# Both ends of the state-space scan in a four-stage token tower: when the second softplus, the last gate, the last products and the output projection are issued

## The chip, the cores and the metric

One of the eight cores of one Trainium2 chip runs the whole kernel. The metric is device time in microseconds (us), the median of several executions. Five engines take part, each with an instruction stream of its own, in order: TensorE (PE in the profile; its weight loads are PEld), VectorE (DVE), ScalarE (ACT), GpSimd (POOL), and SyncE (SP), which only issues transfers here. They meet through semaphores: an instruction adds to one when it is done, and another engine waits until the count is reached.

## The reference, cut to what matters

A tower of five layers over 32 sequences of 64 tokens with 1024 channels. A token layer makes h. Attention, a feed-forward layer with 4-bit weights, a selective state-space layer and a router with low-rank experts are then each added to h. The change touches the state-space layer alone, and the final store of the output:

```
proj = layernorm(h) @ W_in.T ; u, gate = split(proj)          # 2048 channels each
u = silu(conv4(u) + conv_b)
dt, B, C = split(u @ Wx.T) ; each rms-normed                   # 64, 16, 16
delta = softplus(dt @ Wdt.T + dt_bias)
for every token t, channel d and state n (16):
    state = exp(delta * A) * state + (delta * u) * B[n]
    y[t, d] += state * C[n]
y = (y + u * D) * silu(gate)
h = h + y @ W_out.T
```

## The kernel before, in words

The tokens are worked on in four blocks of 512 tokens (nblk = 4, loop over b on each engine). A tile has 128 channels on the partitions and 512 tokens along the row. The state-space layer of a block has four stretches.

*Input projection and gate strips.* A weight strip (1024 x 128) is loaded by SP into one of two raw buffers. ScalarE rounds it to a high part wh (`split`, L642), GpSimd subtracts to get the low part wl (L522), and TensorE makes 24 matmuls of it: high by high, low by high, high by low (`strip`, L947). There are four slots for split strips, so the split of strip i waits until strip i - 4 is used up. Strips WIN0.. make u; strips GATE0..GATE0+15 make the sixteen gate tiles. For gate tile m, VectorE scales psg[m % 2] by rstd in place (L1771), ScalarE takes the Silu into gt[m % 2] (L819) and stores gt to the DRAM tensor `gates` (L822), and strip m of TensorE waits until gate m - 2 has left its bank. Between the gates ScalarE does other work at fixed tiles m. That is soft(0), the softplus of channel tile 0, at m = 7; the diagonal at 9; settled(0), the copy of delta, at 10; transposed(0) at 11; and decay(0, 0) and decay(0, 1), the exponentials, at 12 and 14. Exponentials and the Silu are in different tables, so a switch of tables (ACT_TABLE_LOAD) stands on each side. The delta matmuls (`delta`) of tiles 0 and 1 are issued by TensorE at m = 7 and m = 11.

*The scan.* Sixteen channel tiles m, each with eight steps g (two of the sixteen states in each step). Step g: TensorE puts the drive terms into psx (`drives`, L1198; two buffers, so drives of step g + 1 wait for the scan of g - 1). VectorE runs the recurrence (`scan`, L1746) over 1024 columns from dA and psx into wst. GpSimd multiplies wst by C (L561). TensorE sums over the states into psg banks 0 and 1 (`sums`, L1214), three steps behind the drives. dA and wst have three slots of two steps (RING = 3), so scans wait for ScalarE's decay (L784) and for the sums of six steps before. Between its scans VectorE does soft_sum(m + 1) and drive_sum(m + 1), four small operations (L1718, L1719, L1728, L1729), on what ScalarE's soft(m + 1) (L737 to L744) wrote. When all sums of m are in, ScalarE copies them to twin (`parts`, L775), TensorE folds the two halves together (`finals`, L1233), ScalarE copies the result to u (`summed`), and GpSimd multiplies by the gate that SP loaded back (`gated`, L553). The last tile's gate product is VectorE's (L1735).

*Output projection.* When all sixteen gated tiles are there, ScalarE rounds them to yh (L869), VectorE subtracts to get yl (L1790), and TensorE makes eight output tiles, each from two strips: `strip_over_two` for the even ones (L1017, L1022), two calls of `strip` for the odd ones. VectorE adds each to h (L1796). yh[0..7] lie over the matrices dgB that the drives read, yh[8..15] over dA slots 0 and 1, yl[0..3] over dA slot 2 and yl[4..15] over the three slots of wst. gt lies over one of the two buffers of twin and one of gin.

*Order.* Every stream is written out by hand; there is no planner. The SP queue loads strips, then waits for all gates to be stored, then alternates gin and wdt loads. After the last product it loads h back (2 MB). At the end of the kernel one transfer of 2 MB stores the last block's h (L510).

## Time and profile before

| | us |
|---|---|
| median of 3 runs (lowest, highest) | 4074.54 (4069.95, 4077.92) |
| the profiled execution, device time | 4075.14 |
| its span, first to last instruction | 4073.3 |
| PE busy | 3868.0 (95%) |
| DVE busy | 2674.6 (66%) |
| POOL busy | 2235.6 (55%) |
| ACT busy | 2057.9 (51%) |
| mean granted TensorE clock | 0.983 of full |

The span is the time from the first to the last instruction; 1.8 us of the device time lie around it. Busy shares are means over stretches with different limits. In the projections TensorE never stops, while in the scan TensorE, VectorE and GpSimd are all close to full and take turns at holding the others up. So the places to read are the two seams, from the gate strips into the scan and from the scan into the output projection, which come four times each.

### The profile page before, as it was taken

To read this page: it belongs to the slowest core of one execution; us is meant where nothing else is said; L and a number is where in the kernel's file an instruction comes from. 1 tells how busy PE (TensorE), PEld (TensorE's weight loads), DVE (VectorE), ACT (ScalarE), POOL (GpSimd) and SP (SyncE) were. 2 spreads that over 40 slices of the span, in tenths; PEclk is the share of its full clock that TensorE was granted. 3 is DMA by queue.
4 is the path that set the end of the run, shared out by engine and by line. 5 is a ranking of instruction groups with operands and counts; after the bars stand their busy time and mean duration, and the time that the engine had idled before them with its cause. 6 is when DMAs were issued, how large, how long until landed. Compare 5 with 4: busy or idle time off the path is not lost.

```text
span 4073.3 us, 59277 instructions
## 1 busy us (share of the span) xinstructions
PE 3868.0 (95%) x22816; PEld 2542.0 (62%) x22816; DVE 2674.6 (66%) x2922; ACT 2057.9 (51%) x3012; POOL 2235.6 (55%) x972
## 2 busy tenths in 40 slices
PE   4899999999999999999999999999999999999998
PEld 1568777444678777544577877644377877744466
DVE  6965562999356563799635565499835557299943
ACT  7842344777232343777433233577633234477732
POOL 0023343999533343799733434599943443389952
PEclk7999999999999999999999999999999999999999
DMA  4242234000322224200132223400132223400022
GB/s 113 78 145 83 83 113 158 10 16 15 116 99 84 73 92 153 71 16 16 66 108 99 83 68 122 143 13 16 40 109 99 78 88 104 157 29 16 15 85 73
DMA packets 96697, 320.18 MB, mean 79 GB/s; under 512 B 12353, under 2 KB 16705, under 8 KB 91841
## 3 DMA queue, kind: packets, MB, share of 16 engines
q1 hardware_dynamic: 80320, 275.70, 20.6%
q10 hardware_dynamic: 16128, 41.03, 3.0%
q8 instruction: 173, 2.83, 0.3%
q14 instruction: 76, 0.61, 0.1%
HBM read 272.51 MB, written 44.17 MB: 78 GB/s over the span
## 4 chain that ended last, share of the span: by engine, by line
PE 35%; issue 32%; DVE 20%; POOL 11%; ACT 1%; POOLq 0%; ACTq 0%; DVEq 0%
PE psg L947 20%; DVE sb_wst L1746 17%; POOL sb_wl L522 9%; PE psx L1198 4%; PE psg L1017 3%; POOL sb_wst L561 2%; PE psg L1214 2%; PE psg L1022 1%; PE psx L1246 1%; DVE psg L1719 1%; DVE psg L1718 1%; PE psg L1317 1%; PE psx L964 0%; PE psg L1173 0%; DVE sb_rt L1834 0%
## 5 line engine op out<-in xcount | busy, mean ns | idle before, releaser
L522 POOL TENSOR_TENSOR sb_wl<-sb_raw,sb_wh 128x1024 fp32r<-128x1024 f32 x388 | 959.1, 2476 | 1760.0 <-ACT sb_wh L642 1759.7
L1746 DVE TENSOR_TENSOR_SCAN sb_wst<-sb_dA,psx 128x1024 f32<-128x1024 f32 x512 | 1130.2, 2268 | 9.4 <-PE psx L1198 7.4
L642 ACT ACTIVATE sb_wh<-sb_raw 128x1024 fp32r<-128x1024 f32 x388 | 407.5, 1053 | 558.7 <-PE psg L947 227.6
L784 ACT ACTIVATE sb_dA<-sb_dlt,sb_a_sb 128x504 f32<-128x504 f32 x1024 | 647.0, 705 | 51.8 <-DVE sb_wst L1746 49.6
L1198 PEld LDWEIGHTS psx<-sb_dgB,sb_duT 64*128 64x128 f32 x4096 | 360.4, 188 | 462.5 <-DVE sb_wst L1746 323.4
L1198 PE MATMUL psx<-sb_dgB,sb_duT 64*128 64x256 f32 x4096 | 587.4, 406 | 51.0 <-DVE sb_wst L1746 49.4
L1214 PE MATMUL psg<-sb_wst,sb_cst 64*64 64x512 f32 x4096 | 611.6, 623 | 17.3 <-POOL sb_wst L561 16.4
L561 POOL TENSOR_TENSOR sb_wst<-sb_wst,sb_cb_hi 128x1024 f32<-128x1024 f32 x256 | 596.1, 2362 | 29.9 <-DVE sb_wst L1746 29.5
L561 POOL TENSOR_TENSOR sb_wst<-sb_wst,sb_cb_lo 128x1024 f32<-128x1024 f32 x256 | 600.7, 2371 | 10.6 <-DVE sb_wst L1746 10.2
L947 PE MATMUL psg<-sb_xh,sb_wh 128*128 128x512 f32 x2080 | 532.1, 398 | 12.6 <-POOL sb_wl L522 7.1
L947 PE MATMUL psg<-sb_xh,sb_wl 128*128 128x512 f32 x2080 | 515.6, 390 | 0.0
L947 PE MATMUL psg<-sb_xl,sb_wh 128*128 128x512 f32 x2080 | 514.0, 389 | 0.0
L947 PEld LDWEIGHTS psg<-sb_xh,sb_wh 128*128 128x128 f32 x2080 | 382.6, 188 | 107.1 <-issue 15.3
L947 PEld LDWEIGHTS psg<-sb_xh,sb_wl 128*128 128x128 f32 x2080 | 390.3, 188 | 82.5
L947 PEld LDWEIGHTS psg<-sb_xl,sb_wh 128*128 128x128 f32 x2080 | 390.6, 188 | 81.1
L1214 PEld LDWEIGHTS psg<-sb_wst,sb_cst 64*64 64x64 f32 x4096 | 125.1, 133 | 208.6 <-issue 208.4
L1771 DVE TENSOR_TENSOR psg<-psg,sb_rstd 128x512 f32<-128x512 f32 x64 | 44.8, 700 | 316.0 <-PE psg L947 316.0
L1796 DVE TENSOR_TENSOR sb_h<-sb_h,psg 128x512 f32<-128x512 f32 x32 | 22.0, 688 | 257.3 <-PE psg L947 135.5
L1708 DVE SCALAR_TENSOR_TENSOR sb_cv<-psg,sb_conv,sb_cv 128x504 f32<-128x504 f32 (+2 forms) x192 | 141.0, 735 | 27.8 <-DVE sb_cv L1706 4.1
L775 ACT ACTIVATE sb_twin<-psg 128x512 f32<-128x512 f32 x128 | 69.5, 595 | 172.1 <-PE psg L1222 172.1
L693 ACT ACTIVATE sb_ah<-sb_ao 128x512 fp32r<-128x512 f32 x32 | 20.2, 632 | 193.3 <-DVE sb_ao L1664 193.3
L650 ACT ACTIVATE sb_xh<-sb_xc 128x512 fp32r<-128x512 f32 x128 | 79.1, 618 | 76.5 <-DVE sb_xc L1547 66.6
(274 smaller groups left out, 4959.8 us busy)
## 6 DMA issues: line engine op xcount, KB each, us to landing
sb_raw<-in_w SPq DMA_DIRECT2D x360, 512.0 KB, 3.5
sb_raw<-w_ffn_dequantized SPq DMA_DIRECT2D x32, 512.0 KB, 3.3
gates<-sb_gt ACTq DMA_DIRECT2D x64, 256.0 KB, 2.2
sb_gin<-gates SPq DMA_DIRECT2D x64, 256.0 KB, 2.7
h_after_tok<-sb_h SPq DMA_DIRECT2D x4, 2048.0 KB, 8.9
sb_cb_lo<-c_rows ACTq DMA_DIRECT2D x8, 1024.0 KB, 6.3
sb_cb_hi<-c_rows ACTq DMA_DIRECT2D x8, 1024.0 KB, 7.4
sb_h<-h_after_tok SPq DMA_DIRECT2D x4, 2048.0 KB, 7.7
```

The costliest lines, as they stand in the source:

```text
L522: pool.tensor_tensor(rest(b, i0), raw[:, i0 % RAW, :, :], high(b, i0).bitcast(F32), ALU.subtract).then_inc(s_wl, 1)
L561: pool.tensor_tensor(x, x, cb, ALU.mult).then_inc(s_p, 1)
L642: A(high(b, i0), raw[:, i0 % RAW, :, :], ACT.Copy).then_inc(s_wh, 1)
L650: A(xh[:, k, :], xc[:, k, :], ACT.Copy).then_inc(s_xh, 1)
L775: ins_ = A(twin[:, r, :], psg[:, r, :], ACT.Copy)
L784: ins_ = A(dA[:, (m * NQ + k) % RING, :, n, 1:S], dlt[:, m % 2, :].rearrange("p (b s) -> p b s", b=NB)[:, :, 1:S], ACT.Exp, scale=a_sb[:, ...
L947: ins_ = mm(psg[:, bank, :], w_[:, s_, k, :], x_[:, k0 + k, :], start=start and n == 0, stop=stop_ and n == 3 * KC - 1)
L1017: mm(psg[:, bank, :], w_[:, slot(b, i0 + s), k, :], X[:, k + KC * s, :], start=(k == 0 and n == 0 and s == 0), stop=False)
L1198: ins_ = mm(psx[:, 2 * j + r, :].rearrange("p (a t e) -> p a t e", a=8, e=2)[:, :, :, e], duT[r0:r0 + 64, m % 2, i * P:(i + 1) * P], dgB[r ...
L1214: ins_ = mm(psg[64 * c:64 * c + 64, r, :], C("fold")[r0:r0 + 64, :], wst[r0:r0 + 64, (m * NQ + k) % RING, :, 2 * half + c, :], start=(k == ...
L1708: ins_ = stt(y[:, :, d:S], x[:, :, 0:S - d], tap(3 - d), y[:, :, d:S], ALU.mult, ALU.add)
L1746: v.tensor_tensor_scan(wst[:, x, 4 * j:4 * j + 4, :, :].rearrange("p b n s -> p (b n s)"), dA[:, x, 4 * j:4 * j + 4, :, :].rearrange("p b ...
```

## The change

It does five things.

- VectorE's product. In channel tile 15 the last two C products (TAIL = 2, steps 6 and 7) are made by VectorE after the last scan (`product`, semaphore s_pd), and GpSimd makes six.
- The second softplus. soft(1), settled(1), soft_sum(1) and drive_sum(1) are issued among the gate strips, at m = 12, 14, 13 and 13, rather than in tile 0 of the scan.
- The last gate. The Silu of gate 15 and its store are issued by ScalarE after decay(0, 3), inside the scan. VectorE scales it from PSUM into gt[1], so that its bank is free. VectorE also clears dA's slot 2, which GpSimd did after waiting for the stored gates.
- The output projection. ScalarE copies yh in an order of its own (YH_ORDER) as soon as the drives, and then the scans, are done. TensorE begins the high parts of output tile 0 in bank 3 between the last sums, then does tile 1's highs in bank 1, then both lows. The other six tiles are made by two calls of `strip` each, in a loop.
- The store. The last block's h is stored in four transfers of two tiles each as the tiles are finished.

```diff
+YH_ORDER = list(range(KC)) + [12, 13, 8, 9, 10, 11, 14, 15]
+YL_ORDER = [0, 1, 2, 3, 8, 9, 10, 11, 12, 13, 4, 5, 6, 7, 14, 15]
+YH_AT = {k: n for n, k in enumerate(YH_ORDER)}
+YL_AT = {k: n for n, k in enumerate(YL_ORDER)}
+TAIL = 2
...
+                    for m in range(2):
+                        sp.wait_ge(s_dm, b * DC + m + 1 + CR_DM)
+                        sp.dma_start(wdt[:, m, :], ins["wdt"][m + 2]).then_inc(s_wdt[m], 16)
...
-                        if m < DC - 2:
+                        if 2 <= m < DC - 2:
...
-                    sp.wait_ge(s_p, b * DC * G + DC * G)
+                    sp.wait_ge(s_p, (b + 1) * (DC * G - TAIL))
...
+                if stop >= 5 and b == nblk - 1:
+                    for m in range(0, KC, 2):
+                        sp.wait_ge(s_upd, b * UPDS + 24 + m + 2 + CR_UPD)
+                        sp.dma_start(out[b, :, m:m + 2, :], h[:, m:m + 2, :]).then_inc(s_out, 16)
...
-                    for q in range(2):
-                        pool.wait_ge(s_gst[q], b * (16 * (DC // 2)) + 16 * (DC // 2) + 16)
                     pool.wait_ge(s_cb, 16 * NQ * (b + 1))
-                    settle(pool)
-                    pool.memset(dA[:, 2:RING, :, :, :].rearrange("p k b n s -> p (k b n) s")[:, :, 0:1], 0.0).then_inc(s_z, 1)
                     def gated(m):
...
-                        for g in range(G):
+                        for g in range(G - TAIL if m == DC - 1 else G):
...
+                    pool.wait_ge(s_pd, (b + 1) * TAIL)
...
+                    def gate(m, x):
                         act.wait_ge(s_gr, b * DC + m + 1)
                         act.wait_ge(s_gst[m % 2], b * 16 * (DC // 2) + m // 2 * 16 + 16)
-                        A(gt[:, m % 2, :], psg[:, m % 2, :], ACT.Silu).then_inc(s_gt, 1)
+                        A(gt[:, m % 2, :], x, ACT.Silu).then_inc(s_gt, 1)
                         act.wait_ge(s_gt, b * DC + m + 1 + CR_GT)
                         settle(act)
                         act.dma_start(gates[b, m], gt[:, m % 2, :]).then_inc(s_gst[m % 2], 16)
+                    for m in range(DC):
...
+                        if m < DC - 1:
+                            gate(m, psg[:, m % 2, :])
...
-                        if m in (12, 14):
+                        if m == 12:
                             act.preload_act_table_set(LN_EXP)
+                            soft(1)
                             act.wait_ge(s_zr, b + 1)
-                            decay(0, m // 2 - 6)
-                    act.preload_act_table_set(LN_EXP)
+                            decay(0, 0)
+                        if m == 14:
+                            act.preload_act_table_set(LN_EXP)
+                            settled(1)
+                            decay(0, 1)
                     for m in range(DC):
-                        if m < DC - 1:
+                        if 1 <= m < DC - 1:
                             soft(m + 1)
                         if m == 0:
                             act.wait_ge(s_z, b + 1)
                         decay(m, 2)
+                        if m == 1:
+                            for q in range(2):
+                                act.wait_ge(s_gst[q], b * (16 * (DC // 2)) + 16 * (DC // 2) + 16)
                         if m >= 1:
                             parts(m - 1)
                         decay(m, 3)
+                        if m == 0:
+                            gate(DC - 1, gt[:, 1, :])
+                            act.preload_act_table_set(LN_EXP)
+                        if 1 <= m < DC - 1:
+                            settled(m + 1)
                         if m < DC - 1:
-                            settled(m + 1)
                             decay(m + 1, 0)
                             transposed(m + 1)
                             decay(m + 1, 1)
...
                                 summed(m - 1)
                             diagonal(m + 1)
                     summed(DC - 2)
+                    def y_high(ms):
+                        for m in ms:
+                            act.wait_ge(s_y, b * DC + m + 1 + CR_Y)
+                            A(yh[:, m, :], u[:, m, :], ACT.Copy).then_inc(s_yh, 1)
+                    act.wait_ge(s_ur, (b + 1) * DC * G)
+                    y_high(YH_ORDER[0:10])
+                    act.wait_ge(s_scan, (b + 1) * DC * G + CR_SCAN)
+                    y_high(YH_ORDER[10:14])
+                    split(b, WOUT0 + AHEAD)
+                    y_high(YH_ORDER[14:15])
                     parts(DC - 1)
-                    act.wait_ge(s_y, (b + 1) * DC + CR_Y)
-                    for m in range(DC):
-                        A(yh[:, m, :], u[:, m, :], ACT.Copy).then_inc(s_yh, 1)
-                    for i in range(WOUT0 + AHEAD, BASE0 + 2 if stop >= 5 else LA0):
+                    y_high(YH_ORDER[15:16])
+                    for i in range(WOUT0 + AHEAD + 1, BASE0 + 2 if stop >= 5 else LA0):
...
+                            if k == 0 and m == 0:
+                                pe.wait_ge(s_gt, b * DC + DC - 1 + CR_GT)
+                            if m == DC - 1 and k == NQ - 1:
+                                pe.wait_ge(s_pd, (b + 1) * TAIL)
+                            else:
+                                pe.wait_ge(s_p, b * (DC * G - TAIL) + m * G + 2 * k + 2)
...
+                    def out_highs(m, bank, ks):
+                        for k in ks:
+                            i = WOUT0 + 2 * m + k // KC
+                            if k in (YH_ORDER[0], YH_ORDER[KC]):
+                                pe.wait_ge(s_wl, b * NSTRIP + i + 1 + CR_WL)
+                            pe.wait_ge(s_yh, b * DC + YH_AT[k] + 1)
+                            for n, w_ in enumerate((wh, wl)):
+                                mm(psg[:, bank, :], w_[:, slot(b, i), k % KC, :], yh[:, k, :],
+                                   start=(k == YH_ORDER[0] and n == 0), stop=False)
+                    def out_lows(m, bank):
+                        for k in range(DC):
+                            pe.wait_ge(s_yl, b * DC + YL_AT[k] + 1)
+                            ins_ = mm(psg[:, bank, :], wh[:, slot(b, WOUT0 + 2 * m + k // KC), k % KC, :], yl[:, k, :],
+                                      start=False, stop=(k == DC - 1))
+                            if k % KC == KC - 1:
+                                ins_.then_inc(s_strip, 1)
...
+                            if g == G - 1 and m == DC - 1:
+                                out_highs(0, 3, YH_ORDER[0:4])
                             sums_due(m * G + g - 3)
                             if g == 4 and m < DC - 1:
                                 transposes(m + 1)
                             if g == 4 and m >= 1:
                                 finals(m - 1, m < DC - 1)
-                    for step in range(DC * G - 3, DC * G):
+                    sums_due(DC * G - 3)
+                    out_highs(0, 3, YH_ORDER[4:5])
+                    for step in range(DC * G - 2, DC * G):
                         sums_due(step)
+                    out_highs(0, 3, YH_ORDER[5:8])
                     pe.wait_ge(s_yc, b * (DC - 1) + DC - 1)
                     finals(DC - 1, False)
-                    with loop(pe, 4) as jj:
+                    out_highs(0, 3, YH_ORDER[8:16])
+                    out_highs(1, 1, YH_ORDER)
+                    out_lows(0, 3)
+                    out_lows(1, 1)
+                    settle(pe)
+                    with pe.Fori(1, 4) as jj:
                         for q in range(2):
                             upd(b, 16 + jj * 2 + q - 1)
-                            if q == 0:
-                                strip_over_two(b, WOUT0, jj, 0, yh, yl,
-                                           (lambda k: pe.wait_ge(s_yh, b * DC + k + 1),
-                                            lambda k: pe.wait_ge(s_yl, b * DC + k + 1)))
-                            else:
-                                strip(b, WOUT0 + 2, jj, q, yh, yl, True, False)
-                                strip(b, WOUT0 + 3, jj, q, yh, yl, False, True, KC)
+                            strip(b, WOUT0 + 2 * q, jj, q, yh, yl, True, False)
+                            strip(b, WOUT0 + 2 * q + 1, jj, q, yh, yl, False, True, KC)
...
+                        if m < DC - 1:
+                            tt(psg[:, m % 2, :], psg[:, m % 2, :], rstd[:, :], ALU.mult).then_inc(s_gr, 1)
+                        else:
+                            v.memset(dA[:, 2:RING, :, :, :].rearrange("p k b n s -> p (k b n) s")[:, :, 0:1], 0.0).then_inc(s_z, 1)
+                            v.wait_ge(s_gst[1], b * 16 * (DC // 2) + m // 2 * 16 + 16)
+                            tt(gt[:, 1, :], psg[:, m % 2, :], rstd[:, :], ALU.mult).then_inc(s_gr, 1)
                         if m == 3:
                             prm_norm()
                         if m == 5:
...
                             v.memset(dA[:, 0:2, :, :, :].rearrange("p k b n s -> p (k b n) s")[:, :, 0:1], 0.0).then_inc(s_zr, 1)
                             soft_sum(0)
                             drive_sum(0)
+                        if m == 13:
+                            soft_sum(1)
+                            drive_sum(1)
                     for m in range(DC):
                         for g in range(G):
                             scan(m, g)
-                            if g == 1 and m < DC - 1:
+                            if g == 1 and 1 <= m < DC - 1:
                                 soft_sum(m + 1)
-                            if g == 3 and m < DC - 1:
+                            if g == 3 and 1 <= m < DC - 1:
                                 drive_sum(m + 1)
+                    def product(g):
+                        x = wst[:, (DC * NQ - 1) % RING, 4 * (g % 2):4 * (g % 2) + 4, :, :].rearrange("p b n s -> p (b n s)")
+                        cb = cb_hi[:, 1, 4 * (g % 2):4 * (g % 2) + 4, :, :].rearrange("p b n s -> p (b n s)")
+                        v.wait_ge(s_scan, b * DC * G + (DC - 1) * G + g + 1 + CR_SCAN)
+                        tt(x, x, cb, ALU.mult).then_inc(s_pd, 1)
+                    def y_low(ks):
+                        for k in ks:
+                            v.wait_ge(s_yh, b * DC + YH_AT[k] + 1)
+                            tt(yl[:, k, :], u[:, k, :], yh[:, k, :].bitcast(F32), ALU.subtract).then_inc(s_yl, 1)
+                    v.wait_ge(s_p, (b + 1) * (DC * G - TAIL))
+                    for g in range(G - TAIL, G):
+                        product(g)
+                    y_low(YL_ORDER[0:4])
+                    v.wait_ge(s_acc, (b + 1) * DC * NQ - 2)
+                    y_low(YL_ORDER[4:8])
+                    v.wait_ge(s_y, b * DC + DC - 1 + CR_Y)
                     gated(DC - 1)
-                    for m in range(DC):
-                        v.wait_ge(s_yh, b * DC + m + 1)
-                        tt(yl[:, m, :], u[:, m, :], yh[:, m, :].bitcast(F32), ALU.subtract).then_inc(s_yl, 1)
+                    v.wait_ge(s_acc, (b + 1) * DC * NQ)
+                    y_low(YL_ORDER[8:16])
...
-                        tt(hk(m), hk(m), psg[:, m % 2, :], ALU.add).then_inc(s_upd, 1)
+                        tt(hk(m), hk(m), psg[:, m % 2 if m else 3, :], ALU.add).then_inc(s_upd, 1)
```

## Rows read from the trace of the kernel before

**Rows 1.** The page: shares of the chain that ended last, by engine.

```profile
PE 35%; issue 32%; DVE 20%; POOL 11%; ACT 1%; POOLq 0%; ACTq 0%; DVEq 0%
```

**Rows 2.** Timeline, scan start of block 0, VectorE: start, us, what, [idle before <-releaser].

```profile
703.19 0.70 DVE L1771 TENSOR_TENSOR psg<-psg,sb_rstd 128x512 f32<-128x512 f32 x1 [4.74 <-PE psg L947]
704.26 4.46 DVE L1746 TENSOR_TENSOR_SCAN sb_wst<-sb_dA,psx 128x1024 f32<-128x1024 f32 x2 [0.37 <-PE psx L1198]
710.63 0.70 DVE L1718 SCALAR_TENSOR_TENSOR psg<-sb_spt,psg 128x512 f32<-128x512 f32 x1 [1.91 <-ACT sb_spt L742]
...
722.57 6.64 DVE L1746 TENSOR_TENSOR_SCAN sb_wst<-sb_dA,psx 128x1024 f32<-128x1024 f32 x3 [0.32 <-PE psx L1198]
729.67 2.29 DVE L1746 TENSOR_TENSOR_SCAN sb_wst<-sb_dA,psx 128x1024 f32<-128x1024 f32 x1 [0.45 <-PE psx L1198]
```

**Rows 3.** Timeline of the same stretch, ScalarE.

```profile
688.66 1.28 ACT L842 ACT_TABLE_LOAD   x1 [0.46 <-ACT sb_gt L819]
...
692.40 1.04 ACT L642 ACTIVATE sb_wh<-sb_raw 128x1024 fp32r<-128x1024 f32 x1
...
694.76 0.60 ACT L819 ACTIVATE sb_gt<-psg 128x512 f32<-128x512 f32 x1
...
707.99 0.69 ACT L737 ACTIVATE sb_spt<-psg,sb_conv 128x512 f32<-128x512 f32 x1
...
711.17 4.94 ACT L784 ACTIVATE sb_dA<-sb_dlt,sb_a_sb 128x504 f32<-128x504 f32 x8
```

**Rows 4.** Timeline of the same stretch, TensorE.

```profile
697.55 1.98 PE L947 MATMUL psg<-sb_xh,sb_wh 128*128 128x512 f32 x8
...
714.43 2.08 PE L1198 MATMUL psx<-sb_dgB,sb_duT 64*128 64x256 f32 x8 [3.58 <-DVE sb_wst L1746]
```

**Rows 5.** Windows: stretch, length, busy us of PE, PEld, DVE, ACT, POOL, PEclk, DMA, GB/s.

```profile
709.00:719.00 10.00, 6.42 (x28) 3.01 (x30) 8.26 (x7) 8.08 (x14) 8.74 (x4) 0.50 0.24 60
...
1033.00:1036.00 3.00, 2.49 (x12) 0.89 (x16) 0.00 (x0) 0.00 (x0) 1.59 (x2) 0.50 0.57 131
```

**Rows 6.** Timeline, scan end of block 0: VectorE and GpSimd.

```profile
1024.38 4.46 DVE L1746 TENSOR_TENSOR_SCAN sb_wst<-sb_dA,psx 128x1024 f32<-128x1024 f32 x2 [0.52 <-PE psx L1198]
1039.70 0.69 DVE L1735 TENSOR_TENSOR sb_u<-psg,sb_gin 128x512 f32<-128x512 f32 x1 [10.85 <-PE psg L1233]
...
1024.12 9.25 POOL L561 TENSOR_TENSOR sb_wst<-sb_wst,sb_cb_hi 128x1024 f32<-128x1024 f32 x4
...
1049.90 5.52 POOL L522 TENSOR_TENSOR sb_wl<-sb_raw,sb_wh 128x1024 fp32r<-128x1024 f32 x2 [15.31 <-ACT sb_wh L642]
```

**Rows 7.** Timeline, scan end of block 0: ScalarE.

```profile
1037.36 1.08 ACT L775 ACTIVATE sb_twin<-psg 128x512 f32<-128x512 f32 x2 [13.44 <-PE psg L1222]
1040.43 8.45 ACT L869 ACTIVATE sb_yh<-sb_u 128x512 fp32r<-128x512 f32 x16 [1.99 <-DVE sb_u L1735]
```

**Rows 8.** Timeline, scan end of block 0: TensorE.

```profile
1025.32 1.14 PE L1198 MATMUL psx<-sb_dgB,sb_duT 64*128 64x256 f32 x8
...
1028.91 1.95 PE L1214 MATMUL psg<-sb_wst,sb_cst 64*64 64x512 f32 x16 [1.44 <-POOL sb_wst L561]
1033.51 3.35 PE L1214 MATMUL psg<-sb_wst,sb_cst 64*64 64x512 f32 x16 [2.66 <-POOL sb_wst L561]
...
1041.20 0.47 PE L1017 MATMUL psg<-sb_yh,sb_wh 128*128 128x512 f32 x1 [1.54 <-ACT sb_yh L869]
...
1053.12 1.98 PE L947 MATMUL psg<-sb_yh,sb_wh 128*128 128x512 f32 x8
...
1064.00 0.39 PE L1017 MATMUL psg<-sb_yh,sb_wh 128*128 128x512 f32 x1
```

**Rows 9.** Groups by shape: VectorE's product of two SBUF tiles of 1024 columns.

```profile
L1525 DVE TENSOR_TENSOR sb_low<-sb_low,sb_low_im 128x1024 f32<-128x1024 f32 x8 | 9.8, 1225 | 0.3
```

**Rows 10.** Transfers: the last store's issue; the page's 512 KB load, issue to landing.

```profile
4066.60 0.34 SPq L510 DMA_DIRECT2D out<-sb_h  x1
...
sb_raw<-in_w SPq DMA_DIRECT2D x360, 512.0 KB, 3.5
```

31 lines of the change are left out of this document (8 added, 23 removed).

## The prediction, as it was put on record

> **What bounds the kernel now.** I read the page's chain first. TensorE holds about a third of it, "issue" another, VectorE and GpSimd the rest [rows 1]. So the kernel is bound by TensorE in the projections and by a ring of VectorE, GpSimd and TensorE in the scan, and a shorter seam between the two is paid back in full. Then the timelines of the two seams in block 0; blocks 1 to 3 repeat them within 0.1 to 0.4 us, so a saving counts four times.
>
> At the scan's start VectorE makes two scans and then stands for 1.91 us until ScalarE's second softplus arrives [rows 2]. That softplus is late because ScalarE first does gate 15 and two table loads: it begins at 707.99, and its next operation at 711.17, so it takes 3.2 us [rows 3]. The ninth scan (step 0 of tile 1) is the last of the merged three that begin at 722.57, two scan pitches of 2.19 us on, at 726.95: 22.7 us after the first at 704.26 [rows 2]. A pitch of 2.19 is what 6.64 us for three and 4.46 us for two give.
>
> At the scan's end the last scan ends at 1028.84, and GpSimd's last product at 1033.37, because it makes four in 9.25 us [rows 6]. TensorE waits 2.66 us for the last two, then sums them in 3.35 us, where the two steps before took 1.95 us [rows 8]: the granted clock is 0.50 from 1033 to 1036, its 1.2 GHz level [rows 5]. Then come the twin copies (1.08 us), the last gate product, and only then yh, so the first matmul of the output projection starts at 1041.20 [rows 6 to 8]. Its first two output tiles are done when the third begins, at 1064.00 [rows 8], 35.2 us after the last scan.
>
> **The change, part by part.** All times in the clock of block 0.
>
> *Gate strips, added.* At m = 12 ScalarE does soft(1) between its table load and decay(0, 0): 3.2 us more [rows 3]. The split at 692.40 and gate 13 at 694.76 move by as much, and gate 13 ends at 695.36 + 3.2 = 698.56. TensorE's strip 15 waits for gate 13, and began at 697.55 [rows 4]. So it loses 1.0 us, which is on the path. Bounds: 0, if other work of ScalarE gives way, and the whole 3.2. VectorE's four small operations (0.7 us each) lie beside TensorE's strips, where it idles 4.7 us before each scaling [rows 2]: nothing. settled(1) costs ScalarE 0.6 us at m = 14, where the next thing due, decay(0, 1), is wanted a scan pair after the start: nothing.
>
> *Before the first scan.* VectorE clears a slot (0.1 us) and scales gate 15 (0.70 us, as before [rows 2]). It ended 0.37 us before the drives then, so the scan starts 1.0 to 1.1 us later than before, at about 705.3. The wait on gate 13's store costs nothing: issued at about 699, it has five microseconds until VectorE asks.
>
> *Tile 0 of the scan, removed.* The four operations and the 1.91 us wait go. Eight scans at 2.19 us are 17.5 us to the ninth, where 22.7 were: 5.2 us saved. What is late next? ScalarE: decay(0, 2) can follow the last split at about 706.6 and ends at 709.1, wanted at 714. decay(0, 3) waits for the second scan and ends at 712.3, wanted at 718. Now gate 15 with its two table loads, 1.28 + 0.6 + 0.8 + 1.28, to 716.3. decay(1, 0) to 718.8, wanted at 722.8: four microseconds of cover. transposed(1) to 719.4, wanted by the drives at 721.3. That is the thinnest cover, 1.9 us. GpSimd starts without waiting for the stored gates and ends tile 0 about 3.4 us behind the scans; the next tile's small operations let it catch up. TensorE per step: drives and sums 2.1 us against a scan of 2.19, plus the transposes and delta(2) in tile 0. By steps it is 0.4 us late once, for the tenth scan, as before (0.45 us [rows 2]). So the start seam brings 5.2 - 1.1 = 4.1 us a block.
>
> *TensorE's clock at the scan's start.* In block 0 the granted clock is 0.50 from 709 to 719 [rows 5], and one step's drives take 2.08 us there [rows 4], not 1.14 [rows 8]. Before the change VectorE had its softplus to wait for and hid it. After it a scan every 2.19 us meets 4.1 us of TensorE work per step, twice the 2.1 of full clock. TensorE is idle only for half of each of the first steps now and not for 3.58 us at a stretch [rows 4], so the drop should be rarer and shorter. Bounds: 0, and half of 10 us. I take 0.5 us a block.
>
> *The products.* VectorE's product of 1024 columns from SBUF is nearest to the 1.22 us row [rows 9]; two end at 1028.9 + 2.4 = 1031.3. GpSimd's 2.31 us a piece [rows 6] is the upper bound, which would give 1033.6. The wait for GpSimd's six costs nothing: its sixth ends at 1028.75, the last scan at 1028.84.
>
> *yh early.* The last drives end at 1026.4 [rows 8]. ScalarE's copies go at 8.45 / 16 = 0.53 us [rows 7]: ten to 1031.8, four more to 1033.9, the split to 1035.0, yh 14 to 1035.5, then the twin copies (1.08) to 1036.6. TensorE meanwhile makes four pairs of highs until 1029.2, sums of steps 4 and 5 (1.95 us) to 1031.2, one pair, the last sums at full clock and the diagonal (1.95 + 0.6) to 1034.3, three pairs to 1035.7. So it waits about 1 us for ScalarE, and a VectorE product slower by up to 1.1 us in all would be hidden there. finals end at 1037.7.
>
> *The two first output tiles.* They are 96 matmuls at 0.2267 us (48 in the 10.88 us from 1053.12 to 1064.00 [rows 8]), 21.8 us. Sixteen are done before finals, so 80 are left: 18.1 us. They end at 1037.7 + 18.1 = 1055.8, where it was 1064.0: 8.2 us saved. The inputs keep up. VectorE's last gate product ends at 1038.5 and yh 15 at 1039.1, wanted at 1040.8. The lows are wanted from 1048.5 and ready by 1044. The strips' slots are given back at 1050.3 and 1052.1. With 1.04 us for the split [rows 3] and 2.76 us for the low part (half of 5.52 [rows 6]), strip 4 is ready at 1054.1, wanted at 1055.8; the next at 1056.9, wanted at 1061.2. The load of h, the wdt loads and gate 15's store end far ahead of their readers.
>
> *A rule that speaks against it.* VectorE's yl subtractions read two SBUF tiles while GpSimd works. In the trace GpSimd's two splits beside them took 5.52 us [rows 6], where two of its products of the same size take 4.6 with nothing beside them. The Trainium skill (SBUF — State Buffer, Who interferes with whom) says that such a pair of instructions excludes each other for its whole length. By that rule gated(14) and the split would push VectorE's last gate product by about 2 us, and TensorE would wait 0.3 us in each block; the sum would be 1 us smaller.
>
> *The last store.* It is issued at 4066.60 and the span ends at 4073.3, 6.7 us for 2 MB. Its last quarter alone is nearest to the 3.5 us of a 512 KB load [rows 10]: 3.2 us saved, once. Bounds 0 and 4.5 us.
>
> **Sum.** Four times (4.1 + 8.2 - 0.5) is 47.2, and 3.2 once: 50.4 us. From the profiled 4075.1 that is 4024.7. The median of the runs shown is 0.6 us lower, so I say 4024.
>
> **Rivals.**
> - *TensorE's clock holds the start* (0.13). If each block has 7 to 10 us at the half level among dense steps, each step is 1.9 us short, and TensorE gives back 3.2 to 4.7 us, less 0.4 of slack: the start seam brings nothing, and 47.2 becomes 31 to 37: 4035 to 4041. For it: four drops in four blocks. Against it: they follow stretches of idleness that the change removes.
> - *The end seam is held by ScalarE or the slots* (0.09). If its fifteen copies, split and twin copies run late, or strip 4 is refilled behind TensorE, half of the 8.2 goes: 4 x 4 = 16 us less, 4040.
> - *It does not do what it says* (0.03). yh waits for the drives, and if these end with the last sums nothing overlaps, and the softplus moves its cost to strip 15: within 5 us of 4074. Against it: drives end 2.4 us before the last scan.
> - *Slower: refills become the bound of the output projection* (0.03). The lead of a slot over its reader shrinks from 12.5 to 5.5 us. A pair of strips takes TensorE 10.9 us; a refill chain of load 3.5, split 1.0 and low part 2.8 is 7.3. It decides only when the chain passes 10.9, and costs more than the 11.8 us saved when it passes 12.9 (six pairs at 2 us). At 14 us a pair it would be 18.6 - 11.8 = 6.8 us a block worse: 4098. No row shows such a chain.
>
> **How the numbers follow.** The forecast has 0.72; its own range is 4014 (no stall of strip 15, and a free start) to 4034. With the clock and end rivals that makes 0.94 up to 4042. I leave the rest out and give 4012 to 4042. Within 0.2% is within 8 us of 4074.5, about what a measurement of this kernel can tell from no change. Faster: 0.72 + 0.13 + 0.09 = 0.94; same 0.03; slower 0.03.
>
> **What would show it.** Right: the ninth scan 17.5 to 18 us after the first, no wait for a softplus in tile 0, TensorE idle about 1 us before strip 15, products of 1.2 us, no half clock at the scan's end, third output tile about 27 us after the last scan, the last store under 4 us. Wrong: VectorE idle behind TensorE over several of the first ten scans, TensorE idle of more than 1.5 us before finals, or a wait for wl at the third output tile.

## The result

The changed kernel takes 4029.98 us (median of 4 runs, 4028.57 to 4035.27), the kernel before 4074.58 (4 runs, 4069.95 to 4077.92). The ratio is 0.989, 95% interval 0.9878 to 0.9902: 44.6 us less, where 50.4 were forecast. The profiled execution is the slowest of its four: 4035.27 us with a span of 4033.5, at a granted clock of 0.984.

The program has fixed points that can be read in any of its traces: ScalarE's gate 12, the first, ninth and last scan of each block, and VectorE's second and eighth add into h. From those I made the table below. Each value is a difference of two start times in us (the last scan is taken at its end), blocks 0 to 3 where there are four.

| stretch | before | after |
|---|---|---|
| gate 12 to first scan | 16.66 four times | 17.82 four times |
| first to ninth scan | 22.69, 23.13, 22.74, 23.11 | 18.95, 19.04, 19.02, 19.06 |
| 17th to last scan | 281.1 to 281.2 | 281.1 to 281.2 |
| last scan to second add | 35.35, 35.61, 35.35, 35.54 | 27.08, 27.10, 27.14, 27.14 |
| eighth add to the next block's first gate (three) | 429.54, 430.53, 429.52 | 430.83, 430.86, 430.81 |
| last block's eighth add to the end | 76.78 | 75.74 |
| start to block 0's first gate | 604.18 | 606.89 |

The two seams give 4 x 1.16 - 15.60 - 33.39 = -44.35 us. The last row but one gives -1.04, and the stretches between blocks and before the first gate take 2.9 and 2.7 us more, though the change does not touch them. In sum the profiled span is 39.8 us shorter. The first stretch is not the change's either: it was 596 to 607 us long in the fourteen profiles of this study.

The start of the scan in block 0, VectorE's timeline of the changed kernel (start, us, what, idle before and its releaser), against [rows 2]:

```profile
707.10 0.65 DVE L1828 TENSOR_TENSOR sb_gt<-psg,sb_rstd 128x512 f32<-128x512 f32 x1 [5.94 <-issue]
...
708.14 11.11 DVE L1798 TENSOR_TENSOR_SCAN sb_wst<-sb_dA,psx 128x1024 f32<-128x1024 f32 x5 [0.38 <-PE psx L1220]
719.94 2.29 DVE L1798 TENSOR_TENSOR_SCAN sb_wst<-sb_dA,psx 128x1024 f32<-128x1024 f32 x1 [0.69 <-PE psx L1220]
722.70 6.64 DVE L1798 TENSOR_TENSOR_SCAN sb_wst<-sb_dA,psx 128x1024 f32<-128x1024 f32 x3 [0.48 <-PE psx L1220]
729.80 2.29 DVE L1798 TENSOR_TENSOR_SCAN sb_wst<-sb_dA,psx 128x1024 f32<-128x1024 f32 x1 [0.45 <-PE psx L1220]
```

The softplus wait and the four small operations are gone, and in their place VectorE stands twice behind TensorE's drives (0.69 and 0.48 us). TensorE's timeline of the same stretch, against [rows 4], and the windows view (length, busy us of PE, PEld, DVE, ACT, POOL, granted clock, DMA share, GB/s), against [rows 5]:

```profile
701.29 2.11 PE L985 MATMUL psg<-sb_xh,sb_wh 128*128 128x512 f32 x8 [0.87 <-ACT sb_gt L831]
...
712.66 4.26 PE L1220 MATMUL psx<-sb_dgB,sb_duT 64*128 64x256 f32 x16 [1.04 <-DVE sb_wst L1798]
716.84 1.99 PE L1241 MATMUL psg<-sb_wst,sb_cst 64*64 64x512 f32 x8
718.76 1.14 PE L1220 MATMUL psx<-sb_dgB,sb_duT 64*128 64x256 f32 x8
```

```profile
712.00:719.00 7.00, 6.24 (x26) 2.92 (x28) 7.00 (x4) 5.80 (x8) 7.00 (x4) 0.52 0.10 37
...
1033.00:1037.00 4.00, 3.49 (x28) 1.74 (x22) 4.00 (x5) 3.45 (x6) 2.03 (x2) 1.00 0.93 387
```

The first row is strip 15 waiting for gate 13. From 712.0 to 718.8 the clock is at its 1.2 GHz level: two steps' drives take 4.26 us and one step's sums 1.99, against 1.14 and 1.09 a step at 2.4 GHz. At the end of the scan (1033 to 1037) it is at full now. That end, VectorE and GpSimd first, against [rows 6]:

```profile
1024.52 4.46 DVE L1798 TENSOR_TENSOR_SCAN sb_wst<-sb_dA,psx 128x1024 f32<-128x1024 f32 x2 [0.52 <-PE psx L1220]
1028.98 2.36 DVE L1853 TENSOR_TENSOR sb_wst<-sb_wst,sb_cb_hi 128x1024 f32<-128x1024 f32 x2
1031.26 8.16 DVE L1859 TENSOR_TENSOR sb_yl<-sb_u,sb_yh 128x512 fp32r<-128x512 f32 x8
1039.34 0.68 DVE L1787 TENSOR_TENSOR sb_u<-psg,sb_gin 128x512 f32<-128x512 f32 x1
1039.94 4.89 DVE L1859 TENSOR_TENSOR sb_yl<-sb_u,sb_yh 128x512 fp32r<-128x512 f32 x8
...
1031.42 1.67 POOL L564 TENSOR_TENSOR sb_u<-sb_u,sb_gin 128x512 f32<-128x512 f32 x1 [2.47 <-DVE sb_wst L1853]
1035.05 2.61 POOL L537 TENSOR_TENSOR sb_wl<-sb_raw,sb_wh 128x1024 fp32r<-128x1024 f32 x1 [1.97 <-ACT sb_wh L654]
```

and ScalarE and TensorE, against [rows 7, 8]:

```profile
1026.63 7.39 ACT L898 ACTIVATE sb_yh<-sb_u 128x512 fp32r<-128x512 f32 x14 [2.58 <-PE psx L1220]
...
1035.40 1.05 ACT L787 ACTIVATE sb_twin<-psg 128x512 f32<-128x512 f32 x2
1040.05 0.63 ACT L898 ACTIVATE sb_yh<-sb_u 128x512 fp32r<-128x512 f32 x1 [3.60 <-DVE sb_u L1787]
...
1029.58 1.95 PE L1241 MATMUL psg<-sb_wst,sb_cst 64*64 64x512 f32 x16
...
1032.12 1.95 PE L1241 MATMUL psg<-sb_wst,sb_cst 64*64 64x512 f32 x16
...
1036.60 1.08 PE L1260 MATMUL psg<-sb_twin,sb_cst 128*64 128x512 f32 x4 [0.51 <-ACT sb_twin L787]
...
1055.87 1.98 PE L985 MATMUL psg<-sb_yh,sb_wh 128*128 128x512 f32 x8
```

TensorE has no gap over 0.6 us from the last scan to the third output tile. One thing stands out: VectorE's first eight yl take 8.16 us, the second eight 4.89. The first run beside GpSimd. Taken one by one, six of them last 0.68 us as the others do; the two that meet GpSimd's instructions (1.67 and 2.61 us) last 1.77 and 2.85.

The last store, the queue's timeline and the transfer table, against [rows 10]:

```profile
4005.33 25.46 SPq L519 DMA_DIRECT2D out<-sb_h  x4
...
out<-sb_h SPq DMA_DIRECT2D x4, 512.0 KB, 2.6
```

Four stores are issued in turn. The last is issued at 4030.46 and lands 2.63 us later; the single store of 2 MB landed 6.31 us after its issue at 4066.60.

### The profile page after: what moved, and what is told of

It reads as the page before. It is cut to its first block, busy times and chain, and to the rows that moved or that the text cites. A ratio compares the mean times of both kernels' runs of the same rounds, so it can differ in the third digit from the quotient of the medians.

```text
span 4033.5 us, 59248 instructions
## 1 busy us (share of the span) xinstructions
PE 3869.3 (96%) x22816; PEld 2547.3 (63%) x22816; DVE 2690.4 (67%) x2934; ACT 2057.1 (51%) x3012; POOL 2212.4 (55%) x960
## 4 chain that ended last, share of the span: by engine, by line
PE 36%; issue 32%; DVE 20%; POOL 9%; ACT 2%; POOLq 0%; ACTq 0%; DVEq 0%
PE psg L985 22%; DVE sb_wst L1798 17%; POOL sb_wl L537 9%; PE psx L1220 5%; PE psg L1241 3%; PE psx L1293 1%; PE psg L1271 1%; DVE psg L1771 1%; DVE psg L1770 1%; PE psg L1369 1%; PE psg L1278 1%; ACT sb_yh L898 1%; PE psx L1002 0%; PE psg L1260 0%; PE psg L1195 0%
## 5 line engine op out<-in xcount | busy, mean ns | idle before, releaser
L1220 PE MATMUL psx<-sb_dgB,sb_duT 64*128 64x256 f32 x4096 | 587.5, 406 | 35.3 <-DVE sb_wst L1798 33.3
L572 POOL TENSOR_TENSOR sb_wst<-sb_wst,sb_cb_hi 128x1024 f32<-128x1024 f32 x248 | 577.6, 2365 | 24.7 <-DVE sb_wst L1798 24.7
```

The lines of the kernel that those rows point to most:

```text
L572: pool.tensor_tensor(x, x, cb, ALU.mult).then_inc(s_p, 1)
L1220: ins_ = mm(psx[:, 2 * j + r, :].rearrange("p (a t e) -> p a t e", a=8, e=2)[:, :, :, e], duT[r0:r0 + 64, m % 2, i * P:(i + 1) * P], dgB[r ...
```

## The experiments

Each kernel was timed beside the kernel before, whose median was 4074.19, 4074.58 or 4074.89 us in the three groups of runs. Differences of 1 to 4 us are read from the fixed points rather than from medians, because the runs of one kernel spread over 2 to 10 us. Where the program of a stretch is the same, gate 12 to scan 1 and the end repeat within 0.1 us. The first to ninth scan repeats within 0.4 as long as the clock falls there.

| kernel | median us (lowest, highest) | gate 12 to scan 1 | scan 1 to 9, by block | last scan to second add |
|---|---|---|---|---|
| changed, again | 4030.21 (4029.55, 4034.18) | 17.83 | 18.75, 18.95, 18.95, 19.00 | 27.10 to 27.18 |
| end only | 4034.46 (4029.93, 4039.24) | 16.66 | 22.93, 22.28, 22.91, 22.29 | 27.10 to 27.12 |
| gate kept | 4031.76 (4029.74, 4035.33) | 17.84 | 19.06, 19.07, 19.03, 19.07 | 27.11 to 27.18 |
| extra matmuls | 4019.57 (4017.81, 4025.50) | 17.83 | 17.45, 17.44, 17.44, 17.44 | 27.10 to 27.14 |
| decay at tile 14 | 4027.59 (4026.24, 4032.66) | 16.65 | 19.47, 21.15, 21.27, 21.41 | 27.12 |
| both | 4025.54 (4022.29, 4027.16) | 16.66 | 19.47, 21.05, 21.07, 20.96 | 27.12 to 27.15 |
| decay at 14, split late | 4027.83 (4027.43, 4032.23) | 16.66 | 17.45, 19.08, 19.55, 18.75 | 29.24, 30.85, 30.88, 29.29 |
| the same, extra matmuls | 4020.90 (4016.29, 4026.55) | 16.66 | 17.45 four times | 29.27 to 29.31 |
| the same, yl later | 4014.79 (4014.20, 4016.12) | 16.66 | 17.45 four times | 27.09 to 27.13 |
| products on GpSimd | 4033.82 (4030.45, 4036.35) | 17.82 | 19.03, 18.62, 17.44, 18.63 | 29.44, 29.45, 29.42, 29.09 |
| highs late | 4049.52 (4046.54, 4052.18) | 17.85 | 18.74, 19.09, 18.93, 19.07 | 33.70, 32.20, 33.70, 32.19 |
| one store | 4031.01 (one run) | 17.84 | 18.99, 19.04, 19.06, 19.06 | 27.11 to 27.15 |

**The changed kernel again.** No edit.

> The changed kernel itself once more, for a comparison on the same chip with the next one and for a second profile: about 4030. The stretches gate 12 to first scan (17.8), steady scan (281.1) and end (27.1) repeat within 0.1 us; what differs between its blocks and from the first profile is where the half clock falls, between blocks (429.5 or 430.8 us) and in tile 0 of the scan (17.5 to 19.1 us).

It repeats: 17.83, 18.75 to 19.00 and 27.1 us. Block 0, the 18.75, had the low clock for 3.4 us at the scan's start, the other three for 6.8. The stretch between blocks was 430.74 to 430.86 us, three times of three.

**The end without the start.** ScalarE and VectorE issue the softplus of tile 1 and gate 15 where they did before.

```diff
-                        if 1 <= m < DC - 1:
+                        if m < DC - 1:
                             soft(m + 1)
...
-                        if m < DC - 1:
-                            gate(m, psg[:, m % 2, :])
+                        gate(m, psg[:, m % 2, :])
...
```

VectorE's four operations go back to tile 0 in the same way.

> The scan's start is put back as it was (softplus of tile 1 in tile 0 of the scan, gate 15 among the gate strips), the end and the last store stay changed. If the two seams are independent: gate 12 to first scan 16.7 us and first to ninth scan 22.7 to 23.1 us as before, last scan to the second add into h 27.1 us, so 4 x 8.3 + 3.6 = 37 us less than the kernel before: 4037, and the start part is worth (22.9 - 19.0) - 1.16 = 2.7 us a block. Rival, that part of the end seam's saving comes from GpSimd entering the scan earlier: the end stretch here would be longer than 27.1 us by more than 0.5 us.

Who waited for whom, VectorE, 700 to 735 us (us in total, times, longest):

```profile
DVE psg L1765 <- ACT sb_spt L754: 1.9, 1, 1.9
DVE sb_wst L1793 <- PE psx L1215: 1.2, 3, 0.5
```

The softplus wait of [rows 2] is back, the start stretches are 0.2 us longer than before or 0.8 us shorter, and the end is 27.1 us: the seams are independent. The start part is worth (22.6 - 19.0) - 1.16 = 2.4 us a block against this kernel, 2.7 against the kernel before. The medians are 4.5 us apart with overlapping runs, so they only agree in sign. In the profiled executions of the two kernels the seams differ by 9.7 us. Of these, 5.1 are made up between blocks and behind the last one, where this kernel kept the full clock more often.

**Gate 15 left in the strips.**

```diff
-                        if m < DC - 1:
-                            gate(m, psg[:, m % 2, :])
+                        gate(m, psg[:, m % 2, :])
...
+                    act.preload_act_table_set(LN_EXP)
...
                         if m == 0:
-                            gate(DC - 1, gt[:, 1, :])
-                            act.preload_act_table_set(LN_EXP)
```

> The changed kernel with gate 15 left among the gate strips, from PSUM, so that only the softplus is moved. By the queue of ScalarE: gate 15 ends 3 us after strip 15, decay(0, 2) ends at about 7 us after the first scan, wanted at 8.8, decay(0, 3) at 9.6, wanted at 13: no VectorE wait, first to ninth scan 19.0 as in the changed kernel, or up to 0.3 less; moving the last gate brings nothing by itself. Rival: decay(0, 2) is late and the stretch grows by 1 to 3 us.

All stretches equal those of the changed kernel. Moving the last gate brings and costs nothing.

**Extra matmuls in TensorE's gaps at the scan's start.** Their result is not read.

```diff
                                 drives(m, g + 1)
+                                if m == 0 and g in (0, 1, 2):
+                                    mm(psg[:, 3, :], C("ident"), u[:, 0, :], start=True, stop=True)
```

> The changed kernel with one extra matmul of 512 columns in each of TensorE's three gaps of about 1 us at the start of each scan (its result goes to an idle bank and is not read). Theory 1, TensorE's clock: the 1.2 us that VectorE stands behind the drives in tile 0 (0.69 and 0.48 us in block 0) comes from the half clock of 712 to 719 us; with the gaps filled the clock stays at full, and the first to ninth scan takes 17.6 to 18.0 us instead of 19.0: 4 us less in all. Theory 2, order: the drives queue behind sums that wait for GpSimd, whose first product is held by a late strip split; then the stretch stays within 0.2 us of 19.0, or grows by up to 0.5 us since the extra matmuls stand in front of the drives.

VectorE and TensorE, block 2:

```profile
2587.13 19.71 DVE L1800 TENSOR_TENSOR_SCAN sb_wst<-sb_dA,psx 128x1024 f32<-128x1024 f32 x9 [0.38 <-PE psx L1220]
2607.24 2.29 DVE L1800 TENSOR_TENSOR_SCAN sb_wst<-sb_dA,psx 128x1024 f32<-128x1024 f32 x1 [0.41 <-PE psx L1220]
...
2587.87 1.12 PE L1331 MATMUL psg<-sb_u,sb_cst 128*128 128x512 f32 x2
```

Nine scans without a gap: 17.44 us to the ninth in all blocks, and no half clock in any scan. Theory 1 holds: 1.5 us a block were TensorE's clock. The same time without the extra matmuls, in a block that happened to keep the full clock, says that it is the clock and nothing else in them. It is block 2 of the kernel with all products on GpSimd, whose scan start is the changed kernel's:

```profile
2594.32 19.71 DVE L1797 TENSOR_TENSOR_SCAN sb_wst<-sb_dA,psx 128x1024 f32<-128x1024 f32 x9 [0.38 <-PE psx L1219]
```

That kernel's other blocks had the low clock for 3.4 us (18.62) or 6.8 us (19.03). Adding work to an engine that is near its limit made the kernel faster; the median is 10 us under the changed kernel's, of which 4 x 1.55 = 6.2 are this stretch. Most of the rest is the half clock between blocks, which fell in none of the three here (429.5 us each).

**decay(0, 0) two gate tiles later.** The edit takes it from m == 12 to m == 14, ahead of settled(1).

> The changed kernel with decay(0, 0) moved from gate tile 12 to gate tile 14. Gate 13 then comes 2.5 us earlier and TensorE's 0.87 us wait before strip 15 goes: gate 12 to first scan 16.9 us instead of 17.8, the rest unchanged, 3.6 us less in all (4026). Rival: decay(0, 1) or decay(0, 2) comes too late for the scan (VectorE idle behind ScalarE in tile 0) and the 0.9 us come back there.

TensorE's wait before strip 15 goes, 1.17 us a block. But 0.5 to 2.4 us come back, more than in either theory. VectorE, GpSimd and TensorE, block 2:

```profile
2609.56 2.29 DVE L1798 TENSOR_TENSOR_SCAN sb_wst<-sb_dA,psx 128x1024 f32<-128x1024 f32 x1 [3.14 <-PE psx L1220]
...
2598.46 2.36 POOL L537 TENSOR_TENSOR sb_wl<-sb_raw,sb_wh 128x1024 fp32r<-128x1024 f32 x1 [7.12 <-ACT sb_wh L654]
2600.78 9.29 POOL L572 TENSOR_TENSOR sb_wst<-sb_wst,sb_cb_lo 128x1024 f32<-128x1024 f32 x4
...
2605.55 1.98 PE L1241 MATMUL psg<-sb_wst,sb_cst 64*64 64x512 f32 x8 [1.70 <-issue]
```

ScalarE was not late with dA. It was late with a weight strip's split that stands ahead of its decays. GpSimd, in order, makes that strip's low part before its first product, so the product starts 5.35 us after the first scan (at 2595.43). TensorE's first sums wait for it (the row says issue, but GpSimd's second product ends at 2605.45), and the next drives stand behind the sums. The clock falls in all four blocks, for 3.4 us in block 0 and 6.8 to 10.2 in the others. The seams of this kernel are 2.6 us longer in sum than the changed kernel's, and yet its median is 2.4 us lower: between blocks and behind the last it kept the full clock more often, which was worth 5.0 us in the profiles.

**Both together.** The two edits above in one kernel.

> Both of the above: extra matmuls in the three gaps and decay(0, 0) at gate tile 14. If clock and strip 15 are separate terms: 0.9 + 1.1 = 2.0 us a block, 8 us in all, 4022. If theory 2 holds, only the 3.6 us of the moved decay. If ScalarE becomes the bound when both waits are gone: less than the sum of the two, with VectorE idle behind dA.

The two gains do not add: the stretch is 19.5 to 21.1 us, since the queue on GpSimd comes first. Block 0 kept the full clock and took 19.47, so the queue alone costs 2.0 us over 17.45. In the other three the clock fell for 3.4 us in spite of the extra matmuls, just after TensorE had waited 2.3 us for GpSimd's product, and they took 1.5 to 1.6 us more. All three readings of the expectation fail in size; the bound was neither ScalarE's decay nor the strips.

**The strip's split moved to the scan's end.** To the edit of decay(0, 0):

```diff
-                    splits(b, WOUT0, WOUT0 + AHEAD)
+                    splits(b, WOUT0, WOUT0 + AHEAD - 1)
...
-                    splits(b, WOUT0 + AHEAD, WOUT0 + 4)
+                    splits(b, WOUT0 + AHEAD - 1, WOUT0 + 4)
...
-                        split(b, GATE0 + AHEAD + m)
+                        if m < DC - 1:
+                            split(b, GATE0 + AHEAD + m)
...
-                    split(b, WOUT0 + AHEAD)
+                    split(b, WOUT0 + AHEAD - 1)
                     y_high(YH_ORDER[14:15])
                     parts(DC - 1)
+                    split(b, WOUT0 + AHEAD)
```

> The changed kernel with decay(0, 0) at gate tile 14 as in e6_decay14, and the split of output strip 2 (ScalarE's rounding and GpSimd's subtraction) taken from gate tile 15 to the end of the scan, without extra matmuls. In e6 GpSimd's first product began 5.35 us after the first scan because that split stood before it, TensorE waited 1.7 us for it with the next drives queued behind, and the first to ninth scan took 19.5 to 21.4 us. Queue theory: with the split gone the first product starts 2.3 us after the first scan, TensorE's wait goes, and the stretch falls to 18.0 to 19.2 us, with gate 12 to first scan at 16.7. Rival, clock alone: the half level stays as in e6 and the stretch stays above 20 us in three blocks of four. The end stretch: 27.1 us, or up to 1 us more if the second split there is late for the output projection.

VectorE and GpSimd, block 0:

```profile
704.55 17.51 DVE L1800 TENSOR_TENSOR_SCAN sb_wst<-sb_dA,psx 128x1024 f32<-128x1024 f32 x8
...
704.78 9.31 POOL L572 TENSOR_TENSOR sb_wst<-sb_wst,sb_cb_lo 128x1024 f32<-128x1024 f32 x4 [6.54 <-DVE sb_wst L1800]
```

The first product starts 2.4 us after the first scan (at 702.34). Block 0 had no low clock and reaches 17.45 without extra matmuls; the three others had it and take 1.3 to 2.1 us more. So queue and clock are two causes, shown apart. The end, however, got 2.1 us longer where I had allowed 1, and in two blocks 3.7 with a half clock there.

**With the extra matmuls again.**

> As e9_split_late, with the three extra matmuls per scan start of e5_warm. Queue and clock both removed: gate 12 to first scan 16.7, first to ninth scan 17.4 to 17.6, end 27.1 us: 1.16 + 1.5 = 2.7 us a block less than the changed kernel, 10.6 in all, about 4019, and it beats e5_warm by 4.6 us. If the extra matmuls now delay the sums (GpSimd is ready sooner), the stretch is up to 0.5 us longer.

17.45 us in all blocks, 29.3 at the end: nothing gained on the extra matmuls alone. What holds the end, in VectorE, GpSimd and TensorE of block 0:

```profile
1017.83 10.38 DVE L1863 TENSOR_TENSOR sb_yl<-sb_u,sb_yh 128x512 fp32r<-128x512 f32 x8
1028.14 0.68 DVE L1791 TENSOR_TENSOR sb_u<-psg,sb_gin 128x512 f32<-128x512 f32 x1
...
1021.62 5.44 POOL L537 TENSOR_TENSOR sb_wl<-sb_raw,sb_wh 128x1024 fp32r<-128x1024 f32 x2 [1.97 <-ACT sb_wh L654]
...
1029.53 0.50 PE L1273 MATMUL psg<-sb_yh,sb_wh 128*128 128x512 f32 x1 [1.86 <-ACT sb_yh L899]
```

With a second strip on GpSimd the eight yl take 10.38 us, and the last gate product behind them comes 3.9 us after finals (1023.17 + 1.08).

**The last gate product before the second four yl.**

```diff
-                    v.wait_ge(s_acc, (b + 1) * DC * NQ - 2)
-                    y_low(YL_ORDER[4:8])
                     v.wait_ge(s_y, b * DC + DC - 1 + CR_Y)
                     gated(DC - 1)
                     v.wait_ge(s_acc, (b + 1) * DC * NQ)
-                    y_low(YL_ORDER[8:16])
+                    y_low(YL_ORDER[4:16])
```

> e10_all, in which VectorE makes the last gate product before the second four yl subtractions. In e10 the end stretch was 29.3 us: GpSimd's two strip subtractions ran beside VectorE's yl (8 in 10.4 us where the same 8 alone take 4.9), so the last gate product came 4 us after finals and TensorE waited 1.9 us for yh 15. Theory, the two engines exclude each other in instructions with two SBUF inputs: with the product first the wait goes, and the end stretch falls to 27.1 to 27.6 us; with 16.7 and 17.45 at the start this is about 8.6 us less than e10: 4012 to 4014, 16 us under the changed kernel. Rival: the yl are now late for the lows (needed some 12 us after finals), and TensorE waits there: 28 us or more.

```profile
1022.38 3.58 DVE L1863 TENSOR_TENSOR sb_yl<-sb_u,sb_yh 128x512 fp32r<-128x512 f32 x4
1028.90 0.69 DVE L1791 TENSOR_TENSOR sb_u<-psg,sb_gin 128x512 f32<-128x512 f32 x1 [2.94 <-issue]
1029.51 8.66 DVE L1863 TENSOR_TENSOR sb_yl<-sb_u,sb_yh 128x512 fp32r<-128x512 f32 x12
...
1026.18 4.83 POOL L537 TENSOR_TENSOR sb_wl<-sb_raw,sb_wh 128x1024 fp32r<-128x1024 f32 x2 [1.97 <-ACT sb_wh L654]
```

The two engines no longer overlap for long: GpSimd's pair takes 4.83 us instead of 5.44, the product waits for finals alone (they end at 1028.81, though the row says issue), and the end is 27.1 us. This version takes 4014.79 us, with no run above 4016.12 where the changed kernel beside it had none under 4029.55. It beats both kernels: ratio to the kernel before 0.9852 (0.9836 to 0.9868), while the changed one had 0.9892 (0.9875 to 0.9908). It is 0.8 us above what I expected; the half clock between blocks came three times of three in its profile.

**All products on GpSimd.** TAIL = 0, and VectorE no longer waits for GpSimd's last products.

> The changed kernel with all products on GpSimd (TAIL = 0); VectorE goes straight to the yl subtractions. Last product at 1033.4 instead of 1031.3 in block 0's clock. Theory, products on the path: the last sums end 2 us later, the twin copies start 0.6 us later, so TensorE's wait for them grows: end stretch 27.1 + 0.8 to 1.8 us. It is worth more if VectorE's subtractions slow GpSimd's last products (two SBUF inputs on both engines): up to 3 us more. Rival: hidden by ScalarE's copies, 27.1 to 27.3 us.

VectorE and TensorE, block 0:

```profile
1022.59 12.90 DVE L1858 TENSOR_TENSOR sb_yl<-sb_u,sb_yh 128x512 fp32r<-128x512 f32 x8
1035.41 0.68 DVE L1786 TENSOR_TENSOR sb_u<-psg,sb_gin 128x512 f32<-128x512 f32 x1
...
1027.45 1.95 PE L1240 MATMUL psg<-sb_wst,sb_cst 64*64 64x512 f32 x16 [1.54 <-POOL sb_wst L572]
...
1036.80 0.50 PE L1270 MATMUL psg<-sb_yh,sb_wh 128*128 128x512 f32 x1 [0.97 <-ACT sb_yh L897]
```

The end is 2.0 to 2.35 us longer. TensorE waits for the products (1.54 us) and again for yh 15 (0.97), because VectorE's yl beside GpSimd's products took 12.90 us. So VectorE's two products account for 2.0 to 2.35 of the 8.35 us; 0.97 of it comes because without them the yl run beside GpSimd's own products.

**No output matmuls among the last sums.**

```diff
                             if g == G - 1 and m == DC - 1:
-                                out_highs(0, 3, YH_ORDER[0:4])
...
-                    out_highs(0, 3, YH_ORDER[4:5])
...
-                    out_highs(0, 3, YH_ORDER[5:8])
...
-                    out_highs(0, 3, YH_ORDER[8:16])
+                    out_highs(0, 3, YH_ORDER)
```

> The changed kernel with no output matmuls among the last sums: all highs of tile 0 after finals; yh and yl are still made early. The 16 matmuls of 3.63 us come back on the path: end stretch 27.1 + 3.6 = 30.7 us. If the gaps left in TensorE's stream bring back the half clock at the last sums (as in the kernel before, 1.4 us), and that is on the path: 31 to 32.2 us. So of the 8.35 us saved at the end, 3.6 to 5 would be the interleaving and the rest yh made early and the products. Rival: TensorE waits for yh anyway, and under 3 us come back.

TensorE in block 0:

```profile
1032.46 1.98 PE L1260 MATMUL psg<-sb_twin,sb_cst 128*64 128x512 f32 x4 [2.75 <-ACT sb_twin L787]
```

The end is 32.2 or 33.7 us. Sixteen matmuls at 0.2267 us account for 3.6 of the 5.1 and 6.6 us, the half clock for the rest: it returned in every block, and finals took 1.98 us instead of 1.08. In block 0 it reached further than I expected, into the first ten output matmuls.

**One store.** The four transfers back to one.

> The changed kernel with the last block's h stored in one transfer of 2 MB. From the last add into h to the end of the span 7.5 us as before, instead of 3.8: 3.6 us more, all else equal.

From the last block's eighth add to the end 79.47 us against 75.75 in the changed kernel beside it: 3.7 us.

## Why the prediction was right, and where it was short

*The end seam* was right in place and size: 8.2 us a block forecast, 8.27, 8.51, 8.21 and 8.40 measured. VectorE's products took 1.18 us each (1.22 forecast), the last sums ran at full clock, ScalarE's fourteen copies at 0.53 us. TensorE waited 0.51 us for the twin copies where I had 1.0. The third output tile started 26.9 us after the last scan, as the sum said.

*The rule against it* (the Trainium skill, SBUF — State Buffer, Who interferes with whom) was borne out by the trace. Eight yl took 8.16 us beside GpSimd and 4.89 without, the lengthening all in the two that met an instruction of GpSimd's, and the last gate product came 1.7 us after finals, where about 2 was forecast. The 0.3 us of TensorE's wait did not appear in the changed kernel. A wait there appeared, of 1.86 us, as soon as GpSimd had one strip more, and one reordering took it away, as the rule would have it.

*Strip 15* cost 0.87 us of wait and 1.16 us up to the scan: 1.1 forecast.

*Tile 0 of the scan.* The removal was right (5.2 us forecast; 22.9 to 17.44 is 5.5 with the clock at full). ScalarE with the last gate and its tables inside the scan, whose cover I worked out as 1.9 us at the thinnest, was indeed no bound: the kernel with the gate kept has the same stretches.

*The step that was mis-sized is TensorE's clock at the scan's start.* I took 0.5 us a block, "rarer and shorter". It was there in all four blocks (6.8 us each in the trace) and cost 1.5 to 1.6 us: 19.0 against 17.44, 4 us more in all than I took. My own sign of being wrong was there too: VectorE stood behind TensorE before three of the first ten scans, and the ninth came 19.0 us after the first, not 17.5 to 18. The rival in which the clock eats the whole seam (3.2 to 4.7 us a block) was too dark, the forecast too bright. My reason, that the drops follow an idleness that the change removes, was half true already in the kernel before. In blocks 1 and 3 the clock fell inside TensorE's long wait, but in blocks 0 and 2 ahead of it, after the shorter gaps alone. In block 2 the low clock begins at 2620.2:

```profile
2617.97 1.14 PE L1198 MATMUL psx<-sb_dgB,sb_duT 64*128 64x256 f32 x8 [1.52 <-DVE sb_wst L1746]
2620.15 2.08 PE L1198 MATMUL psx<-sb_dgB,sb_duT 64*128 64x256 f32 x8 [1.04 <-DVE sb_wst L1746]
2625.81 2.08 PE L1198 MATMUL psx<-sb_dgB,sb_duT 64*128 64x256 f32 x8 [3.58 <-DVE sb_wst L1746]
```

The short gaps of 1.0 to 1.5 us between the first drives are still there after the change, and filling them was enough to hold the full level.

*The half clock elsewhere* I had no term for, and it was the larger miss. The second profile of the changed kernel, whose 4030.27 us lie at the median, shows the whole account against the kernel before. The start seam saved 11.4 us (14.4 forecast), the end seam 33.3 (32.8), and the store 3.7 (3.2), which is 2.0 us less than the 50.4 forecast. Half clock in the stretches between blocks (three of three instead of one of three) took 2.8 us, and in the router of the last block 2.7. The stretch before the first gate was 1.9 us shorter by chance. So the error of the sum came out near 6 us in part by luck; without that stretch it would have been 7.5.

The program is the same between the blocks, and what decides whether the clock falls there stays open. In four profiles (the changed kernel twice, the gate kept, one store) it fell there three times of three. In five others (end only, extra matmuls, decay at 14, both, products on GpSimd) it fell there once in fifteen. The other four changed kernels (split late, the same with extra matmuls, yl later, highs late) had it one, one, three and two times of three. The drops thus seem to go with the version, but only the changed kernel was profiled twice, and no run moved a block's length alone.

*A slip in the range.* The lower end of the forecast's own range, 4014, does not follow from the terms: no wait before strip 15 and the full clock at the start are 4 x 1.6 = 6.4 us, which is 4018.

The slower rival had no sign: between the output strips TensorE did not wait for a low part.

## What to carry to other kernels

A wait that covers a slow stretch of another engine hides its price: before removing the wait, ask what that engine does at the lower clock in the same place. When engines run in order, the cost of a moved piece is what stands behind it in each queue it passes; here one weight split ahead of GpSimd's first product cost 2.0 us a block, more than the 1.17 us of the wait that the move removed. Put long runs of VectorE work that reads two SBUF tiles where GpSimd is idle, and put the one instruction that others wait for ahead of them.

## What the runs showed of the hardware

- Three matmuls of 512 columns (1.12 us each) in gaps of 1.0 to 1.5 us kept TensorE at 2.4 GHz in all twelve scan starts of three kernels. In a fourth kernel, where TensorE also waited 2.3 us for GpSimd behind them, it fell in three of four. Without them it fell to 1.2 GHz in 30 of 32 scan starts with the softplus moved, in the changed kernel for 6.8 us in seven of eight.
- At the scan's start 3.4 us at 1.2 GHz cost 1.2 to 1.3 us and 6.8 us cost 1.5 to 1.6, in kernels with the changed kernel's start. A low stretch of 3.4 us between blocks cost 1.0 to 1.4 us.
- VectorE's subtraction of 512 columns from two SBUF tiles took 0.61 us alone. Eight of them took 4.89 us alone, 8.16 beside 4.3 us of GpSimd work (1.67 + 2.61; six took 0.68 and two 1.77 and 2.85), 10.38 beside 7.1 us (1.66 + 5.44), and 12.90 beside GpSimd's last products, gated(14) and a strip.
- A 512 KB store landed in 2.6 us. The 2 MB stores between blocks landed in 7.2 us, and the last one, with no load beside it, in 6.3.
